# Self-attention over eight images on one core: weights laid out by the host, and the maxima of image 0 in other steps

## The reference

```python
xf = x.reshape(b, c, n)                                   # (8, 128, 1024), fp32
q = jnp.einsum('oc,bcn->bon', Wq, xf) + bq[None, :, None]   # Wq (64, 128)
k = jnp.einsum('oc,bcn->bon', Wk, xf) + bk[None, :, None]   # Wk (64, 128)
v = jnp.einsum('oc,bcn->bon', Wv, xf) + bv[None, :, None]   # Wv (128, 128)
attn = jax.nn.softmax(jnp.einsum('bci,bcj->bij', q, k), axis=-1)
out = jnp.einsum('bcn,bmn->bcm', v, attn).reshape(b, c, h, w)
return gamma * out + x
```

## Time and profile before

| | us |
|---|---|
| median of 3 runs | 233.54 (233.38 to 233.80) |
| the profiled execution | 232.45 |
| its span, first to last instruction | 230.7 |
| TensorE busy in the span | 220.9 (96%) |
| ACT, POOL, DVE busy in the span | 177.6, 189.8, 167.6 |

### The profile page before, as it was taken

How to read it: one execution, slowest core, us unless ns; L and a number is a source line. 1 busy time by engine, 2 the same in 40 slices (tenths; PEclk the granted TensorE clock), 3 DMA queues, 4 the chain that set the end, 5 groups by cost and what they waited for, 6 DMA issues and landing times.

```text
span 230.7 us, 5342 instructions
## 1 busy us (share of the span) xinstructions
PE 220.9 (96%) x1864; PEld 204.6 (89%) x1864; DVE 167.6 (73%) x344; ACT 177.6 (77%) x342; POOL 189.8 (82%) x163
## 2 busy tenths in 40 slices
PE   7899988889999999999999999999999999999994
PEld 5477877779999999999999999999999999999994
DVE  1675878677888778867987778778787777776444
ACT  2588966667888788977887788878888878878980
POOL 8769899377998979988798969989799877798871
PEclk9999999999999999999999999999999999999999
DMA  3751930295305870096503961076301951101011
GB/s 94 207 234 42 205 119 4 44 232 146 130 3 134 185 220 11 2 229 155 171 0 90 225 174 63 2 175 149 139 0 33 230 147 51 47 0 18 31 50 45
DMA packets 17882, 24.43 MB, mean 106 GB/s; under 512 B 9920, under 2 KB 10688, under 8 KB 17856
## 3 DMA queue, kind: packets, MB, share of 16 engines
q1 hardware_dynamic: 17552, 23.96, 40.2%
q10 hardware_dynamic: 304, 0.13, 0.2%
HBM read 8.59 MB, written 4.19 MB: 55 GB/s over the span
## 4 chain that ended last, share of the span: by engine, by line
PE 88%; DVE 5%; DMA 2%; ACT 2%; SPq 1%; issue 1%; ACTq 0%
PE sums L618 25%; PE scores L598 13%; PE sums L632 12%; PE work L554 12%; PE scores L599 12%; PE work L548 5%; DVE neg_max L849 2%; DMA q_lomax<-neg_max_r 1%; DMA w_qk<-in_L_conv_Wk 1%; PE work L542 1%; PE work L543 1%; PE work L541 1%; PE sums L554 1%; PE scores L650 1%; PE sums L537 1%; SPq L378 1%
## 5 line engine op out<-in xcount | busy, mean ns | idle before, releaser
L476 POOL TENSOR_TENSOR weight_lo<-weight,weight_hi 128x512 bf16<-128x512 f32 x97 | 135.2, 1409 | 23.5 <-ACT weight_hi L788 22.7
L785 ACT ACTIVATE weight<-scores 128x512 f32<-128x512 f32 x128 | 76.8, 600 | 12.6 <-PE scores L599 5.2
L849 DVE TENSOR_REDUCE neg_max<-work 128x1 f32<-128x512 f32 x120 | 81.7, 683 | 5.5 <-PE work L554 5.5
L618 PEld LDWEIGHTS sums<-values,weight_hi 128*128 128x128 f32 x504 | 76.8, 189 | 4.9
L618 PE MATMUL sums<-values,weight_hi 128*128 128x258 f32 x504 | 80.7, 282 | 0.0
L788 ACT ACTIVATE weight_hi<-scores 128x512 fp32r<-128x512 f32 x128 | 76.8, 600 | 0.0
L598 PE MATMUL scores<-q_hihi,k_hilo 128*128 128x256 f32 x256 | 71.1, 300 | 1.0 <-DMA q_lomax<-neg_max_r 1.0
L599 PE MATMUL scores<-q_lomax,k_hione 128*128 128x256 f32 x256 | 66.2, 281 | 0.0
L554 PE MATMUL work<-k_hilo,q_hihi 128*128 128x512 f32 x120 | 49.1, 412 | 2.8 <-DVE values L845 1.4
L598 PEld LDWEIGHTS scores<-q_hihi,k_hilo 128*128 128x128 f32 x256 | 48.3, 189 | 2.9 <-DMA q_lomax<-neg_max_r 1.4
L599 PEld LDWEIGHTS scores<-q_lomax,k_hione 128*128 128x128 f32 x256 | 48.4, 189 | 1.0 <-issue 0.5
(11 more groups left out here) (84 smaller groups left out, 153.0 us busy)
## 6 DMA issues: line engine op xcount, KB each, us to landing
x_turned_sb<-in_x_turned SPq DMA_DIRECT2D x8, 512.0 KB, 5.3
out<-y_sb SPq DMA_DIRECT2D x15, 256.0 KB, 2.7
x_sb<-in_x SPq DMA_DIRECT2D x7, 512.0 KB, 4.8
q_hihi<-qk_hi SPq DMA_DIRECT2D x12, 256.0 KB, 4.5
q_lomax<-qk_lo SPq DMA_DIRECT2D x7, 256.0 KB, 5.7
k_hione<-qk_hi SPq DMA_DIRECT2D x7, 256.0 KB, 5.3
k_hilo<-qk_hi SPq DMA_DIRECT2D x6, 256.0 KB, 3.2
k_hilo<-qk_lo SPq DMA_DIRECT2D x6, 256.0 KB, 5.7
```

The source lines that it names most:

```text
L476: pool.tensor_tensor(weight_lo[:, r], weight[:, r], weight_hi[:, r], ALU.subtract).then_inc(weight_lo_pool_done, 1)
L618: last = pe.matmul(sums[:, u % 2 * PAIR + it, 0:VCOLS], weight_hi[:, r, part_tile(kt, it)], values[p][:, key_tile(s, kt)], start=(j == 0 a ...
L785: act.activation(weight[:, r], scores[:, s % 2], ACT.Exp)
L849: dve.reduce_max(neg_max[:, t, h:h + 1], place, AX.X, negate=True).then_inc(neg_max_done, 1)
```

## The change

The host stacks four matrices of 128 by 128 as `w_turned`: Wk's transpose twice, Wq's twice, Wq's beside Wk's, and Wv's transpose; and a 128 by 3 array `biases` with the columns bk over bk, bq over bq, bq over bk. ACT loads the first two matrices as `w_kk_t` and `w_qq_t` (64 KB each) in place of the two 32 KB halves of `w_qk`; SP loads the biases with one DMA, and the other two matrices behind the second half of x. The two weight turns, four of the fourteen keep-busy turns and five copies of DVE are gone. ACT scales Wv from SBUF instead of PSUM, after the wait for Wv, bv and gamma that TensorE had. TensorE and POOL wait for `w_qk_t` where POOL waited for the copies. `EARLY_MAXES` holds the same maxima, with the pairs at steps 5, 7, 9, 10 and 13 instead of 8, 9, 11, 14 and 16.

```diff
-WARM_UP = (10, 4)
+WARM_UP = 10
...
-               7: (2, 0, 1), 8: (2, 1, 2), 9: (2, 3, 2), 10: (2, 5, 1), 11: (2, 6, 2),
-               12: (3, 0, 1), 13: (3, 1, 1), 14: (3, 2, 2), 15: (3, 4, 1), 16: (3, 5, 2), 17: (3, 7, 1)}
+EARLY_MAXES = {0: (1, 1, 1), 1: (1, 2, 1), 2: (1, 3, 1), 3: (1, 4, 1), 4: (1, 5, 1), 5: (1, 6, 2),
+               6: (2, 0, 1), 7: (2, 1, 2), 8: (2, 3, 1), 9: (2, 4, 2), 10: (2, 6, 2),
+               11: (3, 0, 1), 12: (3, 1, 1), 13: (3, 2, 2), 14: (3, 4, 1), 15: (3, 5, 1), 16: (3, 6, 1), 17: (3, 7, 1)}
...
             sp.dma_start(x_sb[:, 0, chunk(0)], x_dram[0][:, chunk(0)]).then_inc(first_x_loaded[0], 16)
-            for half in range(2):
-                sp.dma_start(b_kk[half * HEAD:(half + 1) * HEAD, :],
-                             bk.rearrange("(p a) -> p a", a=1)).then_inc(biases_loaded, 16)
-            for half in range(2):
-                sp.dma_start(b_qq[half * HEAD:(half + 1) * HEAD, :],
-                             bq.rearrange("(p a) -> p a", a=1)).then_inc(biases_loaded, 16)
+            sp.dma_start(all_biases[:, :], biases).then_inc(biases_loaded, 16)
             sp.dma_start(x_sb[:, 0, chunk(1)], x_dram[0][:, chunk(1)]).then_inc(first_x_loaded[1], 16)
-            sp.dma_start(w_v[:, :], Wv).then_inc(rest_loaded, 16)
+            sp.dma_start(w_v_plain[:, :], w_turned[3]).then_inc(rest_loaded, 16)
+            sp.dma_start(w_qk_t[:, :], w_turned[2]).then_inc(w_qk_loaded, 16)
...
-            keep_busy(WARM_UP[0], sums[:, 0])
-            pe.wait_ge(w_qk_loaded, 2 * 16)
-            pe.transpose(bank(0)[:, 0:128], w_qk[:, :], identity[:, :]).then_inc(w_turned, 1)
-            keep_busy(WARM_UP[1], sums[:, 0])
+            keep_busy(WARM_UP, sums[:, 0])
...
-                pe.wait_ge(w_ready, 1 if name[0] == "k" else 3)
+                pe.wait_ge(w_kk_loaded if name[0] == "k" else w_qq_loaded, 16)
...
-            pe.wait_ge(rest_loaded, 3 * 16)
-            pe.transpose(bank(0)[:, 0:128], w_v[:, :], identity[:, :]).then_inc(w_turned, 1)
...
-            act.dma_start(w_qk[0:HEAD, :], Wq).then_inc(w_qk_loaded, 16)
-            act.dma_start(w_qk[HEAD:2 * HEAD, :], Wk).then_inc(w_qk_loaded, 16)
+            act.dma_start(w_kk_t[:, :], w_turned[0]).then_inc(w_kk_loaded, 16)
+            act.dma_start(w_qq_t[:, :], w_turned[1]).then_inc(w_qq_loaded, 16)
...
-            act.wait_ge(w_turned, 2)
-            act.activation(w_v_t[:, :], bank(0)[:, 0:128], ACT.Copy, scale=gamma_col[:, :]).then_inc(w_v_ready, 1)
+            act.wait_ge(rest_loaded, 3 * 16)
+            act.activation(w_v_t[:, :], w_v_plain[:, :], ACT.Copy, scale=gamma_col[:, :]).then_inc(w_v_ready, 1)
...
-            dve.wait_ge(w_turned, 1)
-            dve.tensor_copy(w_kk_t[:, :], turned_twice(slice(HEAD, 2 * HEAD))).then_inc(w_ready, 1)
-            dve.tensor_copy(w_qq_t[:, :], turned_twice(slice(0, HEAD))).then_inc(w_ready, 1)
-            dve.tensor_copy(w_qk_t[:, :], bank(0)[:, 0:2 * HEAD]).then_inc(w_ready, 1)
-            dve.wait_ge(biases_loaded, 4 * 16)
-            dve.tensor_copy(b_qk[0:HEAD, :], b_qq[0:HEAD, :]).then_inc(b_ready, 1)
-            dve.tensor_copy(b_qk[HEAD:2 * HEAD, :], b_kk[HEAD:2 * HEAD, :]).then_inc(b_ready, 1)
+            dve.wait_ge(biases_loaded, 16)
```

More of the change, by code:

```diff
@@ L141, in wait, with attention_program @@
         engine.wait_ge(semaphore, count)
-def attention_program(nc, x, x_turned, Wq, bq, Wk, bk, Wv, bv, gamma, out):
+def attention_program(nc, x, x_turned, w_turned, biases, bv, gamma, out):
     fp32 = mybir.dt.float32
@@ L165, in attention_program @@
         identity_r = sbuf("identity_r", [128, 128], fp32r)
-        w_qk = sbuf("w_qk", [2 * HEAD, CHANNELS], fp32)
-        w_v = sbuf("w_v", [CHANNELS, CHANNELS], fp32)
+        w_v_plain = sbuf("w_v_plain", [CHANNELS, CHANNELS], fp32)
         w_qk_t = sbuf("w_qk_t", [CHANNELS, 2 * HEAD], fp32)
@@ L171, in attention_program @@
         w_v_t = sbuf("w_v_t", [CHANNELS, CHANNELS], fp32)
[L172 to L176, removed]
+        w_kk_t = sbuf("w_kk_t", [CHANNELS, 2 * HEAD], fp32)
+        w_qq_t = sbuf("w_qq_t", [CHANNELS, 2 * HEAD], fp32)
+        all_biases = sbuf("all_biases", [2 * HEAD, 3], fp32)
+        b_kk, b_qq, b_qk = (all_biases[:, i:i + 1] for i in range(3))
         exp_of_identity = sbuf("exp_of_identity", [128, 1], fp32)
@@ L210, in attention_program @@
         work = psum("work", [128, 2 * CHUNK], fp32)
+        w_kk_loaded = sem("w_kk_loaded")
+        w_qq_loaded = sem("w_qq_loaded")
         w_qk_loaded = sem("w_qk_loaded")
@@ L649, in project_first @@
                 pe.wait_ge(first_x_loaded[h], 16)
[L650 removed]
+                pe.matmul(place, (w_kk_t if name[0] == "k" else w_qq_t)[:, :],
                           x_sb[:, 0, chunk(h)], start=True, stop=True).then_inc(first_done, 1)
             for name in FIRST[:3]:
[L654 removed]
+                pe.wait_ge(w_kk_loaded if name[0] == "k" else w_qq_loaded, 16)
                 project_first(name)
@@ L752, in round_qk @@
                     wait_spread_mx(act, n - 1)
-                act.activation(qk_hi[:, chunk(h)], place, ACT.Identity, bias=b_qk[:, :]).then_inc(qk_hi_done, 1)
+                act.activation(qk_hi[:, chunk(h)], place, ACT.Identity, bias=b_qk).then_inc(qk_hi_done, 1)
             def round_x(n, h):
@@ L794, in take_low_sum @@
                 act.activation(low_sum[:, u % 2], sums[:, part_banks(u), 0:CHANNELS], ACT.Copy).then_inc(low_sum_done, 1)
-            act.wait_ge(biases_loaded, 4 * 16)
+            act.wait_ge(biases_loaded, 16)
             def first_k(h):
                 act.wait_ge(first_done, FIRST.index(f"k{h}") + 1)
-                act.activation(k_hilo[0][:, chunk(h)], scores[:, h], ACT.Identity, bias=b_kk[:, :]).then_inc(first_hi_done, 1)
+                act.activation(k_hilo[0][:, chunk(h)], scores[:, h], ACT.Identity, bias=b_kk).then_inc(first_hi_done, 1)
             def first_q(h, place):
                 act.wait_ge(first_done, FIRST.index(f"q{h}") + 1)
-                act.activation(q_hihi[0][:, chunk(h)], place, ACT.Identity, bias=b_qq[:, :]).then_inc(first_hi_done, 1)
+                act.activation(q_hihi[0][:, chunk(h)], place, ACT.Identity, bias=b_qq).then_inc(first_hi_done, 1)
             first_k(0)
@@ L807, in _ @@
             first_k(1)
-            act.activation(q_first[:, :], bank(1)[0:HEAD, :], ACT.Identity, bias=b_qq[0:HEAD, :]).then_inc(first_q_done, 1)
-            act.wait_ge(w_turned, 2)
-            act.activation(w_v_t[:, :], bank(0)[:, 0:128], ACT.Copy, scale=gamma_col[:, :]).then_inc(w_v_ready, 1)
+            act.activation(q_first[:, :], bank(1)[0:HEAD, :], ACT.Identity, bias=all_biases[0:HEAD, 1:2]).then_inc(first_q_done, 1)
+            act.wait_ge(rest_loaded, 3 * 16)
+            act.activation(w_v_t[:, :], w_v_plain[:, :], ACT.Copy, scale=gamma_col[:, :]).then_inc(w_v_ready, 1)
             round_v(0, 0, scores[:, 0])
@@ L839, in rest_of_qk @@
                 dve.wait_ge(qk_hi_done, half_count(n, h))
-                dve.scalar_tensor_tensor(qk_lo[:, chunk(h)], place, b_qk[:, :], qk_hi[:, chunk(h)],
+                dve.scalar_tensor_tensor(qk_lo[:, chunk(h)], place, b_qk, qk_hi[:, chunk(h)],
                                          ALU.add, ALU.subtract).then_inc(qk_lo_done, 1)
@@ L929, in first_lo @@
                 low = slice(HEAD, 2 * HEAD)
-                dve.scalar_tensor_tensor(k_hilo[0][low, chunk(h)], scores[low, h], b_kk[low, :],
+                dve.scalar_tensor_tensor(k_hilo[0][low, chunk(h)], scores[low, h], all_biases[low, 0:1],
                                          k_hilo[0][low, chunk(h)], ALU.add, ALU.subtract).then_inc(first_lo_done, 1)
@@ L952, in _ @@
             dve.wait_ge(first_hi_done, len(FIRST))
-            dve.scalar_tensor_tensor(q_lomax[0][0:HEAD, chunk(1)], bank(0)[0:HEAD, :], b_qq[0:HEAD, :],
+            dve.scalar_tensor_tensor(q_lomax[0][0:HEAD, chunk(1)], bank(0)[0:HEAD, :], all_biases[0:HEAD, 1:2],
                                      q_hihi[0][0:HEAD, chunk(1)], ALU.add, ALU.subtract).then_inc(first_q_rest_done, 1)
@@ L1017 @@
     arrays, args = {}, []
-    given = {name: inputs[name] for name in _INS}
-    tiled = np.asarray(inputs["x"]).reshape(BATCHES, CHANNELS, TILES, TILE)
-    given["x_turned"] = tiled.transpose(0, 3, 2, 1)
-    for name in ["x", "x_turned"] + _INS[1:]:
-        a = np.ascontiguousarray(given[name])
+    given = {name: np.asarray(inputs[name]) for name in _GIVEN}
+    wq, wk, wv = (given[f"L0_conv_W{letter}"].T for letter in "qkv")
+    bq, bk = given["L0_conv_bq"], given["L0_conv_bk"]
+    tiled = given["x"].reshape(BATCHES, CHANNELS, TILES, TILE)
+    laid = {"x": given["x"], "x_turned": tiled.transpose(0, 3, 2, 1),
+            "w_turned": np.stack([np.concatenate(pair, axis=1) for pair in ((wk, wk), (wq, wq), (wq, wk))] + [wv]),
+            "biases": np.stack([np.concatenate(pair) for pair in ((bk, bk), (bq, bq), (bq, bk))], axis=1),
```

(3 more changed lines are left out.)

11 lines of the change are left out of this document (3 added, 8 removed).

## The result

The changed kernel takes 231.92 us (median of 8 runs, 230.97 to 232.25) against 233.25 for the kernel before (8 runs, 232.69 to 233.80): a ratio of 0.994, 95% interval 0.9921 to 0.9959. It is faster by 1.3 us, where 3.2 were forecast, and the time lies 0.02 us above the upper end of the range. The forecast started from 233.54, the median of three runs, which over eight came to 233.25; so the time was missed by 1.6 us and the gain by 1.9. The profiled execution took 231.83, its span 230.0.

A forecast was written before the change was run, and what follows sets the result against it. TensorE was taken to bound the long middle, so only what lies ahead of about 53 us could move. Opening 1.6 plus maxima 1.6 made 3.2 us, off 233.54 giving 230.3 us, range 229.1 to 231.9.

The forecast's parts named there:

- The opening: Start of the kernel up to k1: k0 1.26 us earlier and k1 no longer late, 0.32; 1.6 us gained, bounds 1.1 and 1.9.
- q0 follows k0 after 0.86 us: Opening projections: k0 starts at 3.90 and takes 0.86 us, so q0 starts at 4.76 and k1 is wanted at 5.62.
- rival (d): Opening: TensorE, with fewer turns, pauses for w_kk and does its first work at half clock; slower, 239 us at worst; chance 0.05.
- k0's start: Opening: k0 starts at 3.90 instead of 5.16, set by the end of the ten warm-up turns, 1.26 us earlier.
- the second half of x would no longer be late for k1: Opening: with one bias transfer, x's second half lands at 4.9, ahead of k1's 5.62; another 0.32 us gained.
- The maxima: Image 0's steps: old waits gone, 4.4 us, less new waits, 2.8 us; 1.6 us gained, bounds 0.3 and 2.6.
- all four waits of the earlier trace: TensorE's waits for two V read-outs, one q/k read-out and the row of maxima go: 3.3 us, 4.4 with restarts.
- the new waits: Image 0, steps 7 to 18: five gaps of 0.4, 0.2, 0.2, 0.25 and 0.5 us, 2.8 us with restarts.
- the spread in front of (4,0): Step 18: the maximum (4,0) waits for image 2's spread, 7.6 us after its projection; a gap of 0.5, bounds 0 and 1.0.
- no other place would wait: Image 0's steps: the sum counted five new gaps of TensorE, 1.55 us without restarts, and none elsewhere.
- The hidden parts: Behind the opening: later loads w_v, w_qk_t, b_v and gamma, and POOL's wait for w_qk_t, cost nothing; bounds 0 and 0.3.
- the case of the opening alone: Rival: DVE takes the gain of image 0's maxima back, leaving only the opening's 1.6 us; 231.9 us, chance 0.15.

The follow-up runs named there:

- e2: The changed kernel with the old table of maxima, so the loads and missing turns and copies alone: 232.58 us, 0.9985 of the kernel before.
- e6: The changed kernel with the low weights of step 6 on POOL instead of DVE: 230.73 us, 0.9898 of the kernel before.
- e7: The changed kernel with image 2's second q/k projection and the last pair of maxima in step 12 instead of 13: 231.56 us, 0.9928 of before.
- the held kernels: The kernel before, and the changed kernel with the old table, first DMAs held until TensorE made 51 turns, 26 turns following: 241.08 and 240.50 us.

## Why the prediction was wrong

**The opening, 1.6 forecast, 0.35 measured.** The step that failed is "q0 follows k0 after 0.86 us" and the 0.86 for k0 and k1 with it. Those durations are of a stretch behind the rise of the clock, and the change moves the projections into the stretch ahead of it. Before, filler stood there: the w_qk turn and all but the last two of the fourteen turns ran at the lower level, and nobody waited for their results. What takes its place is work that the chain wants, at 1.7 us a projection. My own rows had it: the ten turns in 2.39 us, the four in 0.71 of the earlier trace rows, and the durations of the single turns, which I didn't look at. I read the clock off the column of the stretches, and wrote that no stretch shows the lower level; that is true of the column only. The rival (d) named the mechanism, with TensorE's pause as its cause and a price that only counts as slower; it came without a pause in the traces of e2, e6 and e7 and took a part of the gain. By the held kernels that part is some 0.7 us.

The other 0.5 is in the restarts (a product that starts from a wait takes longer than one in a stream), which the sum left out in the opening: with the clock up k0 took 1.12 us in the chain instead of 0.86, since it starts from a wait (in the trace of before it follows the turns without one), and the first maximum 0.48 instead of 0.24, behind a wait of 0.1. k0's start itself was right: 3.08 us after the first issue with the clock up, 3.17 forecast. That the second half of x would no longer be late for k1, 0.32 us, held: it landed ahead, and k1 took 0.86 in the chain.

**The maxima, 1.6 forecast, 0.9 to 1.0 measured.** The mechanism held: all four waits of the earlier trace rows went, the row of maxima is in time, and the new waits stand where they were placed, the second of step 7, V, the turn of step 8, q/k of step 10, and the spread in front of (4,0). The sizes were off. Counting from the starts of TensorE's products what lies beyond the usual spacing of the same products between 100 and 200 us, and leaving out the 0.08 behind each group of low sums, TensorE lost some 4.5 us between 24 us and (4,0) before and 3.5 after, where the sum had 4.4 and 2.8. The five new waits that the sum had come to 2.55 with their restarts, a little less than their 2.8. The step that failed is that no other place would wait. The second maximum of step 5 takes the bank of the maxima that ACT writes away as a row, which I had not gone into; of two pairs in the timeline

```profile
25.13 0.93 PE L548 MATMUL work<-k_hilo,q_hihi 128*128 128x512 f32 x2
...
36.30 0.62 PE L548 MATMUL work<-k_hilo,q_hihi 128*128 128x512 f32 x2
```

the one in step 5 takes 0.3 more than that in step 10. The maxima of steps 12 and 15 take the banks of the q/k projections two jobs before them and lose 0.17 and 0.18; the projections had been taken for free since no pair follows them. The rest, some 0.25, lies in gaps of under 0.1. DVE's low weights of step 6 took 1.40 us, where I had left them at the 0.92 of before. They set the wait of step 7, as e6_low6_pool shows, but that wait is 0.78 with its restart where the sum had 0.65, so that of the 0.7 they make 0.1.

**The hidden parts.** w_v, gamma and w_qk_t cost nothing, as said: ACT scaled w_v at 9.27 in both traces, and TensorE wanted it later. The spread landed 7.6 us after the projection, as worked out.

**The range.** Its upper end was the case of the opening alone; both gains came, each at a part of its size, which no case had.

## What to carry to other kernels

Look at the durations of one repeated instruction at the start of a kernel, not only at a clock column: work that is moved ahead of the rise of TensorE's clock takes twice as long there, and removing filler from that stretch gives back less than its length. Where jobs take turns at two banks, go through every wait of the new order, those behind single jobs too. And don't take the duration of an instruction over from the old order: DVE's low weights went from 0.92 to 1.40 us by starting at another moment.

## What the runs showed that was not expected

The level rose at 4.57 to 7.22 us in the profiled executions with turns, with the same opening at 4.57, 4.92, 6.44 and, by the products of e6_low6_pool, between 4.8 and 5.6; without turns, TensorE's first work being at 3.86, it rose at 9.04. What sets the moment within one kernel stays open: six turns more or a start 0.5 us sooner didn't bring it forward measurably.

DVE's low weights, one instruction of one shape, took 0.68 us at 41.60 in the trace of before, and 0.92 there at step 6 and 1.40 in the changed kernel, both beside a product of POOL's (x_lo, 1.74 and 1.30): where the one took less, the other took more. All 62 low weights of DVE in the two traces follow one pattern. Those that begin with no product of POOL's running take 0.68 to 0.69 us; the others end 0.55 to 0.68 us behind the product that was running, so that 0.38 us of it still to come make 0.92, and 0.85 make 1.40. And a product of POOL's that begins beside them takes up to 1.76 instead of 1.28. So the one that starts second waits for the other; that is read off the rows, and no run tried it by itself.
